# A causal mask moved from a TensorE product before the exponential to a GpSimd select behind it

## What is computed

```python
q = _apply_rope(q, cos, sin); k = _apply_rope(k, cos, sin)
scores = jnp.einsum('bhtd,bhsd->bhts', q, k) * scale
out = jax.nn.softmax(jnp.where(causal, scores, NEG), axis=-1) @ v
qp = jnp.einsum('bhtd,hd->bht', q[..., :3], dirs)
kp = jnp.einsum('bhsd,hd->bhs', k[..., :3], dirs)
geo = qp[..., :, None] * kp[..., None, :]
geo_out = jax.nn.softmax(jnp.where(causal, geo, NEG), axis=-1) @ v
out = out + scales * (geo_out - out)
```

## Time and profile before

| | |
|---|---|
| median of 3 runs | 466.85 us (465.57 to 467.7) |
| profiled execution, whole time | 464.53 us |
| its span in the trace | 462.6 us |
| busy, share of the span | PE 83%, DVE 72%, ACT 56%, POOL 33% |
| first phase | about the first 277 us; its steady rounds run from about 75 to 240 us |

### The profile page before, as it was taken

How to read it: one execution, slowest core, us unless ns; L and a number is a source line. 1 busy time by engine, 2 the same in 40 slices (tenths; PEclk the granted TensorE clock), 3 DMA queues, 4 the chain that set the end, 5 groups by cost and what they waited for, 6 DMA issues and landing times. The chain is left out here.

```text
span 462.6 us, 7493 instructions
## 1 busy us (share of the span) xinstructions
PE 383.4 (83%) x2290; PEld 252.8 (55%) x2306; DVE 331.9 (72%) x865; ACT 258.3 (56%) x482; POOL 152.0 (33%) x161
## 2 busy tenths in 40 slices
PE   2578899999999999999997714778999999989795
PEld 1345455565554665555643302456777777768573
DVE  4374769877779787797877362568889898897742
ACT  1133676456775667756575222555675585755642
POOL 1221345334553335443341111133433333332310
PEclk9776999999999999999998566569999999999998
DMA  8930003000000000000000000000000000000001
GB/s 233 314 118 1 0 2 104 11 13 11 14 0 13 12 13 13 12 2 11 13 13 11 0 1 2 0 0 0 3 13 11 24 11 14 13 12 24 11 25 34
DMA packets 13642, 13.14 MB, mean 28 GB/s; under 512 B 2004, under 2 KB 12884, under 8 KB 13476
## 3 DMA queue, kind: packets, MB, share of 16 engines
q1 hardware_dynamic: 13604, 12.67, 9.1%
HBM read 10.57 MB, written 2.10 MB: 27 GB/s over the span
## 5 line engine op out<-in xcount | busy, mean ns | idle before, releaser
L884 POOL TENSOR_TENSOR c_h_lo<-c_hb,c_h_hi 128x512 fp32r<-128x512 f32 x32 | 40.8, 1274 | 72.0 <-ACT c_h_hi L927 66.7
L1022 PE MATMUL wide<-had,c_h_hi 128*128 128x512 f32 x128 | 54.0, 422 | 7.5 <-ACT c_q2T L938 7.5
L1022 PE MATMUL wide<-had,c_h_lo 128*128 128x512 f32 x128 | 51.2, 400 | 0.0
L1008 PE MATMUL wide<-c_q_T,w_tern_all 128*128 128x256 bf16 x256 | 38.3, 292 | 8.3 <-DVE c_hh L1120 6.9
L296 POOL TENSOR_TENSOR a_qk<-a_rot_c,a_rot_s 128x320 f32<-128x320 f32 x16 | 15.4, 962 | 72.6 <-DVE a_rot_s L677 72.6
L302 POOL TENSOR_TENSOR a_split_q<-a_qk,a_split_q 128x256 fp32r<-128x256 f32 x16 | 33.8, 2111 | 15.3 <-ACT a_split_k L394 15.3
L921 ACT ACTIVATE c_sl<-c_z 128x512 f32<-128x512 f32 x32 | 20.1, 628 | 29.4 <-DVE c_z L1111 29.3
L776 DVE TENSOR_TENSOR x_res<-x_res,bank 128x256 f32<-128x256 f32 x16 | 6.8, 422 | 40.9 <-PE bank L597 36.2
L1008 PEld LDWEIGHTS wide<-c_q_T,w_tern_all 128*128 128x128 bf16 x256 | 24.2, 103 | 20.7 <-DVE c_hh L1120 9.3
L586 PE MATMUL bank<-w_o,a_att 128*128 128x256 f32 x128 | 33.3, 405 | 1.9 <-issue 1.1
L563 PE MATMUL wide<-a_g_diag,a_row_sb 40*128 40x512 f32 x64 | 31.7, 615 | 2.6 <-DVE a_g_diag L696 2.6
(11 more groups left out here) (168 smaller groups left out, 1009.6 us busy)
## 6 DMA issues: line engine op xcount, KB each, us to landing
x_res<-in_x SPq DMA_DIRECT2D x4, 512.0 KB, 6.2
b_vT<-in_ctxT SPq DMA_DIRECT2D x16, 128.0 KB, 2.3
out<-c_yo SPq DMA_DIRECT2D x16, 128.0 KB, 1.7
w_raw_all<-in_wg SPq DMA_DIRECT2D x1, 1024.0 KB, 7.4
w_raw_all<-in_wu SPq DMA_DIRECT2D x1, 1024.0 KB, 9.8
w_raw_all<-in_wd SPq DMA_DIRECT2D x1, 1024.0 KB, 12.3
had_f<-in_h SPq DMA_DIRECT2D x1, 1024.0 KB, 4.9
w_o_raw<-in_Wo SPq DMA_DIRECT2D x4, 128.0 KB, 6.3
```

What stands on the lines that cost most here:

```text
L884: nc.gpsimd.tensor_tensor(h_lo[p][:, j::FQ, :], hb[j % 2][:, :].rearrange("c (m t) -> c m t", m=2), h_hi[p][:, j::FQ, :].bitcast(F32), ALU ...
L1008: mm = nc.tensor.matmul(dst[:, m * TOK:(m + 1) * TOK], w[:, k * FF + blk * P:k * FF + blk * P + P], q_T[p][:, k * TOK:(k + 1) * TOK], star ...
L1022: mm = nc.tensor.matmul(wide[:, 1 + i, m * 512:(m + 1) * 512], a[p][:, j + FQ * m, i * P:(i + 1) * P], had512[:, j, :], start=(j == 0 and ...
```

## The change

The two mask products of L559 go, and L563 starts the accumulation itself. Behind the exponential GpSimd runs a select over the whole tile `e_g` in place: an element stays where t - s >= 0 and becomes 0 elsewhere. TensorE's sums and weighted values now wait for the select's semaphore `gs` and no longer for the exponential's `eg`.

```diff
@@ the semaphores' names
-                     "rab gm gd nm es geo eg pd pn vn ln inv att wo x1").split()
+                     "rab gm gd nm es geo eg gs pd pn vn ln inv att wo x1").split()
@@ GpSimd's body, at its end, behind b_rstd
+                    if m is not None:
+                        u, p = m
+                        need(pool, A["eg"], u + 1)
+                        nc.gpsimd.affine_select(e_g[p][:, :], e_g[p][:, :], [[0, H], [1, P]], ALU.is_ge, 0.0,
+                                                base=0, channel_multiplier=-1).then_inc(A["gs"], 1)
@@ TensorE's body, stage b
                         need(pe, A["es"], u + 1)
-                        need(pe, A["eg"], u + 1)
+                        need(pe, A["gs"], u + 1)
                         need(pe, A["vn"], u + 1)
@@ TensorE's body, stage m
                         need(pe, A["eg"], u)
                         need(pe, B["en"], KC * (u - 1))
-                        for g in range(2):
-                            nc.tensor.matmul(geo[:, g * 512:g * 512 + 512], ident_b[:, :], mask_st[:, :],
-                                             start=True, stop=True)
                         need(pe, A["gd"], u + 1)
                         for g in range(2):
                             mm = nc.tensor.matmul(geo[:, g * 512:g * 512 + 512], k_row[p][:, :],
-                                                  g_diag[p][:, g * 512:g * 512 + 512], start=False, stop=True,
+                                                  g_diag[p][:, g * 512:g * 512 + 512], start=True, stop=True,
                                                   skip_group_check=True)
```

## The result

The changed kernel takes 485.78 us in the median (483.52 to 486.71, 4 runs) against 466.21 of the kernel before in the same comparison: 1.0415 times as long, 95% interval 1.0365 to 1.0465 (below, intervals stand in brackets behind the ratio). A ratio leaves out executions over 1.5% above the fastest of their kernel, so it can differ a little from the quotient of the medians. Its profiled execution took 483.52 us with a span of 481.8, which is 19.2 us more than before. The second phase begins 19.1 us later (296.40 against 277.26, by the first instruction of GpSimd in it) and is as long as it was, so the first phase has all of it.

What follows compares the result with a forecast made beforehand. VectorE's chain early in each steady round was taken to set TensorE's waits, and `g_diag` L563's. Select delays 12.5 + 1.3 less 0.5 made 13.3 us on the profiled 464.53, 477.8; with the median 2.3 above, 480 us, range 467 to 500.

Steps and rivals of the forecast that it cites:

- the select's term: Rounds 4 to 16: the select delays VectorE's `b_xn` and everything behind it by 0.96 us a round, 12.5 us in all.
- The forecast itself: Steady rounds: VectorE held by GpSimd's select with TensorE at full clock, 480 us, own range 475 to 490; chance 56%.
- the prediction's own signs of being wrong: `b_xn` at 0.40 us beside a running select, select over 2.3 us, L552 waiting for `gs`, or steady-round clock below 1.00.
- GpSimd's select holds VectorE, and not the other way round.: Steady rounds: the select starts at 155.92, before `b_xn`, which stands until the select is done; 0.96 us delay.
- the formula: Delay of `b_xn` in a steady round: (155.92 + D + 0.15) - 156.71 = D - 0.64, D being the select's length.
- The length of the select.: GpSimd's select over one tile was taken as 1.6 us, range 1.27 to 2.32, from the subtraction's rows.
- The mask products cost nothing and give nothing back.: Before L563 in steady rounds: the products lie within TensorE's wait for `g_diag`, so removing them was priced at nothing.
- The clock: Rival: waits before L529 lower TensorE's clock in half of thirteen rounds, adding some 12 us, 492 us; chance 20%.
- The last rounds.: Round 17: `b_xn` and L552 end 1.3 us later behind the last select; round 16 gains 0.5 us without mask products.
- The select hidden, too long, or the change faster: Three rivals: select hidden, 466 to 467 us, 13%; select from 3.7 us on, 510 us, 6%; mask time saved, 458 us, 5%.

Runs made afterwards that it cites:

- the first experiment: The changed kernel with the old mask products put back before L563 as idle filling, select still late: 475.02 us, 1.0114 of the kernel before.
- first comparison: The changed kernel (mask products out, select behind `b_rstd`) first timed against the kernel before: 485.78 us against 466.21, ratio 1.0415.

## Why the prediction was right, and what in it was not

The forecast, 480 us with a range of 467 to 500, holds the measured 485.78, and the direction and the place are right. That the sum came so near is in good part luck: the select's term was 7.2 us too large, and the falls of the clock, some 10 us in the ten steady rounds alone, were not in it. The forecast itself, VectorE held at the full clock, is what the late select with the masks kept comes nearest to, and that was 1.1% slower, not the 2.9% of the sum's 13.3 us. Of the prediction's own signs of being wrong, one came true: the granted clock of the steady rounds is 0.93. And the rounds without a fall are 0.41 us longer, not 1.

- *GpSimd's select holds VectorE, and not the other way round.* Right. `b_xn` ends 0.15 us behind the select, as the formula had it; the formula gives 1.09 - 0.64 = 0.45 us, and 0.41 was measured, as the select starts 0.04 us before `b_rstd` ends by the records. No semaphore stands between the two, so the engines meet not only at semaphores. With the select earlier, while VectorE is idle, the hold is gone. The Trainium skill ("SBUF — State Buffer", "Who interferes with whom") says that whichever of the two engines issues first has the shared port pair for its whole instruction; `b_xn`, which ends 0.15 us behind the whole select, agrees. Who has it next went both ways: by turns in the run with two selects, and to VectorE again at L302.
- *The length of the select.* The first term that failed, in size. I took 1.6 us and a lower bound of 1.27, from a two-operand subtraction with the same number of values read. It is 1.093, below the bound. So the term of the steady rounds was 13 x 0.41 = 5.3 us and not 12.5; the first experiment agrees. The estimate of 0.85 us by the Trainium skill ("GPSIMD Engine Reference", 4.1, one-input operations roughly at line rate) was 0.24 too short, where the lower bound from the rows was 0.18 too long.
- *The mask products cost nothing and give nothing back.* Right in the time of the round: L565 and L560 start behind `g_diag` (0.15 us in the round shown, not 0.05), and no round is shorter without them. Wrong in the whole, and the second term that failed, as it was put at nothing: I named their cover, the wait for `g_diag`, and not what they did there. With them TensorE was working in that wait. Taken out alone they cost 1.0%.
- *The clock*, a rival with 20%, came true, at about the size I gave it (12 us for half of the rounds; 6 of 10 at 1.63, and the last rounds). Its cause and place were only half as I had them. I saw the sums L552 at the lower clock behind the longer wait for `m_row`. Where the masks are in, they are what slows down behind such a wait; in the changed kernel it is the output projection, behind the empty gap at L565. The place alone doesn't tell the cause, as the falls of the kernel before, with the masks in, stand there too. The longer wait of 0.59 us alone left two long rounds of ten.
- *The last rounds.* 1.3 - 0.5 us was far too little: the last three intervals have 5.5, as L565 of round 16 (3.78 us) and the output projection behind it run at the lower clock.
- *The select hidden, too long, or the change faster*: none. L557 did not wait for `gs` in a steady round.

What is shown: without the mask products the kernel loses 1.0 to 1.2%, with no select or with one that holds nobody, and with the products in it doesn't; and the late select costs its 0.41 us a round. What stays open: why both together cost 1.3% (first comparison: 2.0%) more than the two apart, and why an execution has two long rounds and another one none with the same program. The table rests on single traces; that more empty time goes with more falls is argued from it, and 3 against 2 is little.

## What to carry to other kernels

Work on an engine that waits anyway isn't always free to remove: on TensorE it may be what keeps the clock up, so before taking it out look at the granted clock of that stretch and at the gaps that would be left. An operation moved to GpSimd should be laid where VectorE has no such work as `b_xn` or the scans to run; moving the select ahead of `b_rstd` gave `b_xn` its 0.40 us back. And where a trace shows the lower clock behind a wait, a handful of idle products into PSUM that nobody reads is a cheap trial: here they gave 1.2 to 1.5%.

## What the runs showed of the hardware

- A GpSimd select over 128 x 1024 float32 in SBUF, in place, takes 1.09 us; a two-operand subtraction over half as many columns took 1.28.
- With the mask products out and no select, the clock fell to 1.2 GHz again and again, though no wait of TensorE that the trace lists in the steady rounds was longer than 0.62 us. One fall makes a round 1.6 to 1.7 us longer where it stands at the output projection, 1.0 to 1.6 at the sums.
- Whether it falls differs between executions of one program: none and two in the two traces of the kernel before.
